# A graph layer on one core: half of a scaling on ScalarE, one stored result a pair, z of chosen nodes made again from base rows

## The reference

```python
xn = _layernorm(x, axis=-1)
x = x + _L0_gnn_ref(xn, edge_index, ...) + _L0_mix_ref(xn[None], ...)[0]
x = x + _L0_ffn_ref(_layernorm(x, axis=-1)[None], ...)[0]
# _L0_ffn_ref(x, ...), cut:
weights = (jnp.einsum('bsd,do->bso', x, wr) + br)[..., 0]
_, idx = jax.lax.top_k(weights, k)
sel_idx = idx[:, :kk]
sel = jnp.take_along_axis(x, sel_idx[:, :, None], axis=1)
h = jax.nn.gelu(jnp.einsum('bkd,dh->bkh', sel, w1) + b1)
y = jnp.einsum('bkh,hd->bkd', h, w2) + b2
y = y * w_sel[..., None]
processed = jnp.zeros_like(x).at[batch_idx, sel_idx].set(y)
return processed + x
```

## Time and profile before

| | us |
|---|---|
| median of 3 timed runs | 3163.41 (3161.61 to 3163.52) |
| the profiled execution, its own time | 3166.19 |
| its span, first to last instruction | 3164.4 |
| mean granted TensorE clock of the span | 0.825 of 2.4 GHz |

### The profile page before, as it was taken

How to read it: one execution, slowest core, us unless ns; L and a number is a source line. 1 busy time by engine, 2 the same in 40 slices (tenths; PEclk the granted TensorE clock), 3 DMA queues, 4 the chain that set the end, 5 groups by cost and what they waited for, 6 DMA issues and landing times.

```text
span 3164.4 us, 38617 instructions
## 1 busy us (share of the span) xinstructions
PE 2127.0 (67%) x8271; PEld 1510.3 (48%) x8271; DVE 1910.4 (60%) x4819; ACT 732.8 (23%) x2199; POOL 2108.6 (67%) x2189
## 2 busy tenths in 40 slices
PE   4557358877766676667767677777764366269998
PEld 3435135544444444444545454555443111168887
DVE  7996458877777777755555555555555688742221
ACT  2225232211111111121112111122210366222222
POOL 4727667777777777777777777777773688044433
PEclk7669679988888888788888888888877677579999
DMA  5537644444444444455555555555543699211111
GB/s 169 155 108 229 114 112 124 128 123 124 124 124 124 125 125 127 132 145 153 153 153 153 153 153 153 155 153 153 152 130 88 171 291 292 82 34 56 55 55 45
DMA packets 259969, 426.67 MB, mean 135 GB/s; under 512 B 73682, under 2 KB 165748, under 8 KB 259764
## 3 DMA queue, kind: packets, MB, share of 16 engines
q0 software_dynamic: 96592, 260.07, 31.7%
q1 hardware_dynamic: 163300, 165.80, 16.5%
HBM read 337.21 MB, written 88.48 MB: 135 GB/s over the span
## 4 chain that ended last, share of the span: by engine, by line
POOL 37%; issue 20%; PE 19%; DVE 16%; DMA 4%; ACT 1%; ACTq 1%; DVEq 1%; POOLq 1%; SPq 0%
POOL G L1234 31%; PE bank L2033 7%; PE bank L916 5%; PE bank L925 5%; DMA G<-tab_d,sidx 4%; POOL rows_d L1218 3%; POOL G L1211 3%; DVE G L1645 2%; DVE G L557 1%; DVE G L553 1%; DVE G L554 1%; DVE acc L1661 1%; DVE G L538 1%; ACT sidxF L1858 1%; ACTq L1854 1%
## 5 line engine op out<-in xcount | busy, mean ns | idle before, releaser
L1234 POOL DMA_INDIRECT G<-tab_d,sidx x1632 | 1549.2, 949 | 518.0 <-issue 479.9
L2033 PE MATMUL bank<-G,ident 128*128 128x264 f32 x3264 | 920.8, 436 | 600.7 <-DVE G L1645 519.7
L2033 PEld LDWEIGHTS bank<-G,ident 128*128 128x128 f32 x3264 | 656.9, 212 | 861.8 <-issue 515.3
L1645 DVE TENSOR_TENSOR G<-G,bank 128x1024 f32<-128x1024 f32 x408 | 491.1, 1214 | 1.8
L1661 DVE TENSOR_TENSOR acc<-acc,bank 128x264 f32 x816 | 347.8, 426 | 193.7 <-PE bank L2033 160.9
L1900 ACT ACTIVATE bank<-work 128x196 f32<-128x196 f32 x51 | 17.2, 338 | 1210.7 <-DVE work L1632 1210.7
L2014 PE MATMUL bank<-kvw,shared 128*128 128x512 f32 x392 | 183.7, 613 | 48.6 <-DVE shared L1563 36.7
L1616 DVE CAST work<-penI 128x64 f32 (+1 forms) x51 | 11.7, 229 | 321.4 <-DMA G<-tab_d,sidx 318.3
L1984 PE MATMUL bank<-G,acc 128*128 128x264 f32 x392 | 136.4, 507 | 95.3 <-DVE acc L1374 73.1
L889 POOL DMA_INDIRECT out<-G,acc x49 | 48.9, 998 | 192.5 <-DVEq L1004 182.9
L916 PE MATMUL bank<-G 128*128 128x256 f32 (+1 forms) x800 | 175.4, 378 | 0.0
(11 more groups left out here) (398 smaller groups left out, 3118.0 us busy)
## 6 DMA issues: line engine op xcount, KB each, us to landing
G<-tab_d,sidx POOLq DMA_INDIRECT x1632
acc<-x_in SPq DMA_DIRECT2D x98, 256.0 KB, 4.0
shared<-xnT_d SPq DMA_DIRECT2D x98, 256.0 KB, 3.9
accP_d<-acc SPq DMA_DIRECT2D x100, 132.0 KB
tab_d<-acc SPq DMA_DIRECT2D x49, 260.0 KB, 3.3
xnT_d<-acc SPq DMA_DIRECT2D x49, 256.0 KB, 2.3
mix_d<-acc SPq DMA_DIRECT2D x49, 256.0 KB, 3.0
G<-mix_d SPq DMA_DIRECT2D x49, 256.0 KB, 4.3
```

Source lines behind the costliest of these rows:

```text
L1234: g.indirect_dma_start(out=G[:, s, t, 0:TR], out_offset=None, in_=tab_d, in_offset=bass.IndirectOffsetOnAxis(ap=sidx[:, s, t:t + 1], axis= ...
L1645: v.tensor_tensor(gm[:, q4], gm[:, q4], W1[:, q4][:, :, :, None].to_broadcast([P, 4, HG, CG]), ALU.mult).then_inc(g_ready, 1)
L2033: last = te.matmul(bank[1 + i % NSB][:, 0:ROW], ident[:, :], G[:, s, i * IT + k, :], start=(k == 0), stop=(k == IT - 1))
```

## The change

What it does, in the order of the stages:

- **z is not stored.** ACT writes only b (new L661), so `z_d` and its store are gone. The router weight is now taken from x2 of the same pair, straight after its statistics (`node_weight(q)`, new L541), and turned into that of z later for all blocks at once: times the inverse deviation, plus shift times the sum of the router's weights (two 128x98 instructions in `threshold_dve`).
- **b = x2 times (1 + inv) + shift.** The sum 1 + inv moves from DVE (the old reduction L568) to ACT (a 128x2 activation, new L654, on which L661 waits). inv, 1 + inv and shift are kept for all 98 blocks.
- **ACT scales half the sums.** POOL's L591 shrinks from 128x512 to 128x256 (new L592). The second block is scaled on ACT by four 128x64 activations, one a head, each with a per-partition scale (`scale_second`, new L628). It stands in ACT's order behind the exponential of the next pair and ahead of the logarithm. PE waits for it before both matmuls of a pair (`sum_scaled`).
- **Denominators of two pairs at once.** `weights_of(g)` covers pairs 2g and 2g+1 and is called in every other step; its three instructions have 16 columns instead of 8. `own_sums` runs six pairs ahead instead of four.
- **z of the chosen rows is made again.** From b and the row's two numbers: z = b * inv/(1+inv) + shift/(1+inv). `threshold_dve` makes the two factors for all blocks (a reciprocal and two products), SP stores them to `norm_d` (2 numbers a node). The gather of z rows now reads `out`, each followed by a gather of 8 bytes a row from `norm_d` by a list `norm_i` of its own; ACT applies them in place (`make_z`, new L998, two activations of 256 columns) before PE turns the rows. `make_z(q+2)` stands in ACT's order ahead of the GELUs of step q. The gather of z for step q+4 is issued behind the scatter of step q and ahead of the gather of b.

The diff, without renamings, buffers and waits at the ends:

```diff
@@ node_dve
-            def weights_of(q):
+            def weights_of(g):
...
+                pairs = range(2 * g, min(2 * g + 2, NP))
...
-                dve.wait_ge(z_ready, q + 1)
                 for t in (0, 1):
-                    wk(v.scalar_tensor_tensor(junk, zz[:, q % 2, t, :], 1.0, wr_ps, ...))
+                    wk(v.scalar_tensor_tensor(junk, x2[:, q % 2, t, :], 1.0, wr_ps, ...))
...
-                if q + 3 < NP:
-                    weights_of(q + 3)
-                if q:
-                    node_weight(q - 1)
+                if q % 2 and q + 3 < NP:
+                    weights_of((q + 3) // 2)
+                node_weight(q)
                 dve.wait_ge(v_std, q + 1)
-                v.tensor_reduce(mv2[:, s, :, 3], mv2[:, s, :, 1:3], AX, ALU.add)
@@ node_pool
-                g.tensor_tensor(heads(uu[:, s]), heads(acc[:, 2 * q:2 * q + 2, 0:D]), wide(rec[:, q % 4]), ALU.mult)
+                g.tensor_tensor(uu[:, s, 0, :].rearrange("p (h n) -> p h n", h=HG), ...)
...
-            for q in range(4):
+            for q in range(6):
                 own_sums(q)
@@ node_pe
                 pe.wait_ge(u_scaled, q + 1)
+                pe.wait_ge(sum_scaled, q + 1)
@@ node_act
+            def scale_second(q):
...
+                for h in range(HG):
+                    last = a.activation(uu[:, q % 2, 1, h * CG:(h + 1) * CG], acc[:, 2 * q + 1, h * CG:(h + 1) * CG], ACT.Copy,
+                                        scale=rec[:, q % 4, 1, h:h + 1])
+                last.then_inc(sum_scaled, 1)
...
                 if q + 1 < NP:
                     exponent(q + 1)
+                if q + 2 < NP:
+                    scale_second(q + 2)
...
+                a.activation(inv1[:, 2 * q:2 * q + 2], inv[:, 2 * q:2 * q + 2], ACT.Identity, bias=1.0).then_inc(inv1_ready, 1)
...
-                    a.activation(zz[:, s, t, :], x2[:, s, t, :], ACT.Identity, ...)
@@ threshold_dve
+            lk(v.tensor_tensor(wnode[:, :], wnode[:, :], inv, ALU.mult))
+            lk(v.scalar_tensor_tensor(wnode[:, :], shift_n, wr_sum, wnode[:, :], ALU.mult, ALU.add))
...
+            lk(v.reciprocal(inv1, inv1))
+            lk(v.tensor_tensor(stat[:, :, 1], shift_n, inv1, ALU.mult))
+            lk(v.tensor_tensor(stat[:, :, 0], inv, inv1, ALU.mult))
...
+            lk(v.scalar_tensor_tensor(norm_i[:, 0:NT2], perm_l, float(NB), bank[6][:, 0:NT2], ALU.mult, ALU.add))
@@ ffn_pool
+            def gather_z(q):
+                gather(zl, out, q, z_in)
+                for t in tiles(q):
+                    g.indirect_dma_start(out=nl[:, q % 2, t, :], out_offset=None, in_=norm_d, ...)
@@ ffn_act
+            def make_z(q, s, u):
+                act.wait_ge(z_in[s], 64 * u + 32 * len(tiles(q)))
+                for t in tiles(q):
+                    last = a.activation(zl[:, s, t, :], zl[:, s, t, :], ACT.Identity, bias=nl[:, s, t, 1:2], scale=nl[:, s, t, 0:1])
+                last.then_inc(z_made, 1)
```

148 lines of the change are left out of this document (89 added, 59 removed).

## The result

The changed kernel takes 3167.1 us (median of 20 runs, 3164.95 to 3170.94), the kernel before beside it 3163.45 (20 runs): a ratio of 1.0014, 95% interval 1.0008 to 1.0020. That is 3.65 us slower; +10.4 was forecast. The total hides larger movements of both signs.

| stage | before | after | difference | forecast |
|---|---|---|---|---|
| up to the first gather of sums | 2472.83 | 2470.27 | -2.6 | 0 |
| start of the node loop | 16.35 | 20.59 | +4.2 | +4.5 |
| node loop, 48 steps | 216.53 | 206.09 | -10.4 | +0.5 |
| to the first gather of the last loop | 87.9 | 87.3 | -0.7 | -0.8 |
| first gather to second turn | 9.1 | 14.9 | +5.7 | +6.2 |

The account below looks back on a forecast made before the run. DVE was taken to pace the node loop and PE the feed-forward loop. Terms +4.5 + 0.5 - 0.8 + 6.2 = +10.4 us gave 3173.8 against the timed median, written 3174; range 3156 to 3206, forecast's own 3166 to 3185.

Parts of the forecast that it names:

- own signs: Node loop: right if PE's first matmul waits for L628, DVE for the exponential ahead of L556, and steps are 4.4-4.7.
- The start of the node loop: Before the node loop: POOL issues 12 gathers instead of 8 ahead of its first scaling, less a halved L591: +4.5 us.
- End and selection: Node loop's end and selection: DVE's wait and weighing of z replaced by shorter work, small additions after it: -0.8 us.
- Start of the last loop: Feed-forward loop's start: PE's second turn waits for the tenth gather instead of the sixth, then for make_z: +6.2 us.
- The steady step: Feed-forward loop: make_z and GELUs free the bank 0.1 us before PE's next up, so no cost: 0.
- The size of the scalings: ACT in the node loop: four 64-column scalings take 1.09 us, one 0.35; bounds for four 0.53 and 1.43.
- The node loop: Node loop, 48 steps: DVE's saving turns into a wait, 217.0 us against 216.5: +0.5 us.
- the mean of the ring: Node loop: closed cycle of exponential, four scalings and PE, 1.80 + T, 4.52 us a step at the mean clock.
- DVE still is the bound: Rival for the node loop: steps stay at DVE's 4.2 us, loop 202, saving 14.5, total 3158.8; chance 0.24.
- weights_of: DVE in the node loop: 0.52 us for two pairs at the same length, 0.26 a step, which saves 0.26.
- The 0.53 for four scalings: Low bound for ACT's scalings in the node loop, from 8-column copies: ring's mean 3.96, DVE's floor of 4.2 holds, -14.5 us.
- The end: From the last scatter to the program's end: no change forecast, 0.

Follow-up runs that it names:

- e6: Changed kernel with each gather of 8-byte factors issued twice, the second into a spare place: ratio 1.0090 to the kernel before.
- e10: Kernel before with 24 more indirect DMAs of GpSimd during the selection, into unused SBUF: one execution, node loop 216.6 us, drain 3.57 us.
- e2: Changed kernel with four more ScalarE activations per pair, ahead of the four the matmul needs: ratio 1.0246 to the kernel before, node loop 279.2 us.
- e4: Changed kernel with only GpSimd's issue order changed at the starts of node loop and last loop: ratio 1.0013 to the kernel before.
- e9: Changed kernel with four pairs of sums issued before the first scaling and a lead of five pairs instead of six: ratio 1.0002 to the kernel before.
- e3: Changed kernel with GpSimd scaling both blocks of a pair and ScalarE none: ratio 1.0031 to the kernel before, node loop 212.0 us.
- e8: Changed kernel with weights_of on one pair, 8 columns, in every step: ratio 1.0044 to the kernel before, node loop 215.1 us.
- e12: Changed kernel with e9's issue order, e1's later PE wait, base rows gathered once, and PE's first up before its second turn: ratio 0.9976 to the kernel before.
- e5: Changed kernel without the 49 gathers of 8-byte factors, z made with fixed scale and shift: ratio 0.9986 to the kernel before, drain 3.57 us.
- e7: Changed kernel with the 49 factor gathers taking 1 KB rows instead of 8 bytes: ratio 1.0017 to the kernel before, drain 7.90 us.
- e1: Changed kernel with PE waiting for ScalarE's scaled sums only ahead of a pair's second matmul: ratio 1.0010 to the kernel before, node loop 205.6 us.
- e11: Changed kernel with GpSimd scaling both blocks and the first instruction of weights_of made a reduction: ratio 1.0027 to the kernel before, node loop 211.4 us.

## Why the prediction was right, and where it was not

The time, 3167, lies inside the range and inside the forecast's own (3166 to 3185), 7 below the forecast, on the predicted side. The working was not as good as that. Two terms were wrong by 10.9 and 4.3 us with opposite signs, and the others were right. Without the 4.3 us at the end, which I had not foreseen, the time would have been 3162.8, still in the stated range but outside the forecast's own; that the forecast looks as close as it does is luck. By its own signs the forecast's mechanism failed: PE's first matmul did wait for L628, but the steps are 4.29 on average and not 4.4 to 4.7, and DVE waited for the exponential ahead of the first L556 alone.

*The start of the node loop*, +4.5: measured +4.24. *End and selection*, -0.8: -0.7. *Start of the last loop*, +6.2: +5.7, since the 8-byte rows land in 2.3 us where I took 2.7. *The steady step*, 0: 0, and e6 shows that the cover was 0.7 us and not 0.1.

*The size of the scalings* was right: 1.05 for four, 0.335 each (326 to 348), forecast 1.09 and 0.35. With exponential and hops they make 1.68 of idle time at PE between pairs, where I had 1.80.

*The node loop*, +0.5, is the step that failed, and in it this sentence: "and then the mean of the ring holds: 4.52 a step". Its T of 2.72 was the mean of the kernel before, and a mean clock was carried over into a schedule that changes what PE does between pairs. It was not even a constant of the old schedule: in e10 the same loop had T = 2.53. In the changed kernel T was 112.93/48 = 2.35, the clock 0.88, and the ring's mean 1.68 + 2.35 = 4.03 is below DVE's floor, so the forecast's wait of every step did not come about. The rival "DVE still is the bound" had named the condition, T under 2.4 with my 1.09, and priced the loop at 202; it came to 206.1. Against it I said that steps of 4.2 us were "hardly another case" than ones of 4.51. The clock says otherwise: 0.88 in all four executions of the new loop. What I had given too little weight is that PE stands idle for a shorter time, mostly 1.7 and not 2.55 us behind a fast pair. That the shorter idle time raised the clock is argued, not shown: longer idle times come with 0.76 to 0.84, and with 0.66 in e2, but e4 and e9, with 1.68 behind most pairs, have 0.82 and 0.84, and none of the runs changed the clock alone.

*weights_of*: 0.52 for two pairs was 0.66 (4.61 - 3.95). The reciprocal of 16 columns takes 254 ns for 204, L534 176 for 157 and L536 176 for 169, 0.08 together; the other 0.06 I can't place. That is 23 x 0.14 = 3.2 us of the 4 by which the loop lies above the rival's 202.

*The rival of GpSimd as a limit* was not among mine, and rightly: with all scalings on it (e3) the loop is still 4.6 shorter than before. But I took its halved scaling to be worth nothing in the loop, and it is worth 5.9, over DVE's two-operand instructions.

*A bound.* The 0.53 for four scalings is the time of four copies of 8 columns. The 56 columns that a scaling has more would add 0.05 each by the slope of L964, so the low bound should have been 0.72. It changes nothing: the ring's mean is 4.15 with it, still under the floor of 4.2.

*The end*, 0: +4.3. I counted the gathers that the change adds where they stand, and not at the program's end.

So of the loop's 10.4 us: 9.0 are gone if weights_of goes back to one pair (e8), 5.9 if GpSimd scales all (e3). They overlap, because only the two-pair form falls into GpSimd's time: in the kernel before, with all scalings on GpSimd and 8 columns, L530 and L532 ran beside a scaling at the start of the loop alone, but for 8 ns once. Against the loop's 10.4 and the selection's 0.7 stand 4.2, 5.7 and 4.3: +3.1.

## What to carry to other kernels

A closed ring through two engines is priced with the clock that the new schedule will be granted, not with the mean of the old one; where floor and ring are within half a microsecond of each other, give both a like chance, and open the ring by putting the wait ahead of the last matmul that needs it: that was worth 0.5 to 1.3 us of the loop with a long lead at its start, and 4.4 with a short one (e9, e12). Work taken from GpSimd can pay on VectorE without any wait in the profile: compare the duration of the same VectorE instruction with GpSimd busy and idle. A start that is made shorter by putting issues off has spent the lead that the steps behind it live on, so price the first ten steps with it, and look at what the last instruction of every engine does when the number of DMAs changes.

## What the hardware showed that I had not expected

- The closing drain of GpSimd took 3.57, 3.57, 7.90 and 3.90 us with 2078, 2102, 2127 and 2176 indirect DMAs in the program, equal to the nanosecond in runs of the same number, and the same for rows of 8 bytes and of 1 KB. In the slower series 2078 gave 4.39. The drain ahead of the node loop (L250) took 11.5 to 12.2 in all.
- A 16-column TENSOR_TENSOR on DVE with both operands in SBUF took up to 0.63 us beside a TENSOR_TENSOR on GpSimd, and 0.18 without; each one that met it ended 0.04 to 0.05 us behind it. One of 8 columns took 4.35 beside four of them (4.33 in e10). A reduction, a reciprocal and instructions with one operand in PSUM were not delayed.
- PE's clock in the node loop, with the median idle time behind a fast pair: 0.88 with 1.8 us (changed kernel, e5, e6, e7), 0.84 with 2.1 (e8), 0.82 with 2.1 (e1), 0.80 and 0.79 with 2.5 (e3, e11), 0.76 and 0.82 with 2.6 (the kernel before, twice), 0.66 with 2.6 behind every pair (e2); but 0.82 and 0.84 with 1.7 in e4 and e9.
- Gathers of 128 rows of 8 bytes landed in 2.2 to 3.2 us (median 2.3), rows of 1 KB beside them in 2.7 to 2.9, and GpSimd issues either every 1.25 us.
